# Linear attention on one Trainium2 core: normalising the queries with channels on partitions instead of tokens on partitions

## The chip, the cores and the metric

One core of a Trainium2 chip runs one program. The metric is the device time of the program in microseconds (us), the median of several runs. TensorE (PE) multiplies, VectorE (DVE), ScalarE (ACT) and GpSimd (POOL) work elementwise, and SyncE (SP) issues the DMAs. Each engine executes its own queue in order and waits on semaphores that the others raise.

## The reference

Four layers on x of 1024 tokens and 256 channels, each x + layernorm(layer(layernorm(x))): softmax attention, a mixture of experts, a gated linear attention, and a second mixture of experts. The change is in the linear attention, which has 16 heads of 128 channels:

```
q = silu(causal_dwconv(hidden @ Wq, qconv_w, qconv_b))      # 4 taps
k = silu(causal_dwconv(hidden @ Wk, kconv_w, kconv_b))
q = layernorm(q.reshape(B, L, H, 128), qn_w, qn_b)           # per token and head, over 128 channels
k = layernorm(k.reshape(B, L, H, 128), kn_w, kn_b)
S_t = (1 - b_t) S_(t-1) + b_t v_t k_t^T                      # b_t = sigmoid(hidden @ Wb + bb)
o_t = S_t q_t
out = (o * silu(hidden @ Wg)) @ Wo
```

## The kernel before

The layers follow each other. The linear attention (class `LinearAttention`) takes the span from about 400 to 774 us. It works head by head. The 1024 tokens are 8 tiles of 128 (`NT = 8`), and the recurrence is computed by tiles: inside a tile by scores, from tile to tile by a state of 128 x 128.

The steps of a head h, and the engine of each:

- `high_q`, `high_k`, `high_gate` (ACT) and `low` (POOL) split the float32 weights in two parts; `project_q`, `project_k`, `project_gate`, `project_v` (PE) multiply both parts, so that a projection of 1024 tokens is 12 matmuls of 512 columns (v: 24 of 256).
- `tap` (ACT) copies a projection out of PSUM with the last tap, and `convolve` (DVE) adds the three others in three instructions. Channels are on partitions here. `silu` (ACT) follows.
- `rows_q` and `rows_k` (PE) transpose the eight tiles, so that tokens are on partitions. `variances` (DVE) takes mean and variance of each token; `power` (POOL) makes the inverse deviation.
- For q, `norm_q` (DVE, eight instructions, L2233) subtracts the mean and multiplies by the inverse deviation out of PSUM, `turn_q` (PE, eight transposes) turns the result back to channels on partitions, and `q_transposed` (ACT, L2043) applies weight and bias and writes `q_T`. For k, `shift_k` (DVE) and `norm_k` (ACT, eight instructions) normalise, `rows_k` of POOL (two instructions of 128 x 1024, L2307 and L2309) makes the rows, `turn_k` and `k_transposed` make `k_T`.
- `mask` (POOL) and `exp_mix` (ACT) prepare the decay inside a tile, `decay_q` and `decay_v` (POOL) scale q and v.
- `score`, `key_values`, `outputs` (PE), `probs`, `states` and `gate` (DVE), `silu_gate` (ACT) compute the head's output. `gate` multiplies `outputs` by the gate.

The order on each engine is written out by hand, as a pipeline over steps n in which heads n, n-1 and n-2 are in work. In the steady part a step is:

- PE: rows_q(n-1), turn_k(n-2), rows_k(n-1), project_gate(n-2), score(n-2), key_values(n-2), project_q(n), project_k(n), project_v(n), turn_q(n-1), outputs(n-2).
- DVE: shift_k(n-1), probs(n-2), states(n-2), convolve q(n), convolve k(n), gate(n-2), variances q(n), variances k(n), norm_q(n).
- POOL: power k(n-1), low q(n), low k(n), low v (even n), mask(n), decay_q(n-2), low gate(n-1), rows_k(n-1), decay_v(n-1), power q(n).
- ACT: high_q(n), k_transposed(n-2), high_k(n), silu_gate(n-2), high_v (even n), exp_mix(n-1), tap q(n), norm_k(n-1), tap k(n), high_gate(n-1), silu q(n), q_transposed(n-1), silu k(n), copy_v(n).

Variances of head n run on DVE in step n, but wait for rows_q(n) and rows_k(n), with which PE begins step n+1. Four pairs of PSUM banks hold everything: pair 3 serves project_q, rows_q and turn_q in turn, pair 1 project_k, turn_k and score, pair 2 rows_k and outputs, pair 0 the gate, v and key_values. The wait in front of a PE step is mostly for such a pair. SP loads weights and the decay rows; at step 3 it issues the whole of `Wo` (2 MB), which the next block needs.

## Time and profile before

| what | value |
|---|---|
| median of 3 runs | 1073.07 us (1071.62 to 1076.11) |
| the profiled execution | 1076.29 us, its span 1074.4 us, granted clock 0.984 |
| busy share of the span: PE, DVE, ACT, POOL | 95%, 72%, 63%, 46% |
| from 600 to 750 us, busy of 150 us: PE, DVE, ACT, POOL | 149.46, 137.52, 119.93, 108.71 us |

The profile is one execution, recorded by the hardware. A busy PE is not PE at its peak, since matmuls overlap in the record; whether PE sets the pace is read from what it and the other engines wait for. In a timeline row, "x8" is eight instructions in one row with their time from first start to last end, and the brackets give how long the engine was idle before the row, and what released it.

### The profile page before, as it was taken

What the parts mean: (1) busy time and instruction counts of PE and PEld (TensorE: products, weight loads), DVE (VectorE), ACT (ScalarE), POOL (GpSimd) and SP (SyncE); (2) the same over time, 40 slices, a digit from 0 to 9 for tenths busy, and PEclk for the clock granted to TensorE, in tenths of its full rate; (3) what the DMA queues carried; (4) which work ended last, traced back from release to release, by engine and by line L of the source; (5) the groups of instructions that cost most, each with busy time, mean ns of one, the idle gap of its engine ahead of it and who ended that gap; (6) DMA issues with size and microseconds to landing.
All of it is one profiled execution on the core that took longest, in us unless ns stands there. A gap on an engine that the chain in (4) does not pass through costs nothing. (4 is left out here: it accounts for less than half of the span.)

```text
span 1074.4 us, 19331 instructions
## 1 busy us (share of the span) xinstructions
PE 1024.1 (95%) x6893; PEld 811.8 (76%) x6893; DVE 778.0 (72%) x1645; ACT 675.7 (63%) x1229; POOL 498.5 (46%) x441
## 2 busy tenths in 40 slices
PE   7999999999999996999999999999799999999997
PEld 4333333467888885899899999999699788888997
DVE  5899999556677647899999999999457465343843
ACT  4588888765453447877788788877445353333454
POOL 3351400113079532777767686777306000437443
PEclk9999999999999999899999999999899999999999
DMA  4443434142234103332222123110001123555100
GB/s 97 87 83 51 85 59 70 47 125 73 70 119 93 34 6 117 101 98 64 78 96 65 56 65 114 59 69 21 19 18 42 45 52 97 159 147 171 59 21 20
DMA packets 80794, 79.31 MB, mean 74 GB/s; under 512 B 29384, under 2 KB 67740, under 8 KB 80700
## 3 DMA queue, kind: packets, MB, share of 16 engines
q1 hardware_dynamic: 79968, 77.14, 27.1%
q10 hardware_dynamic: 732, 0.95, 0.3%
q8 instruction: 55, 0.90, 0.3%
q14 instruction: 39, 0.32, 0.1%
HBM read 65.51 MB, written 1.28 MB: 62 GB/s over the span
## 5 line engine op out<-in xcount | busy, mean ns | idle before, releaser
L744 ACT ACTIVATE attn_probs<-attn_rows_k 128x512 f32<-128x512 f32 x256 | 138.9, 595 | 24.1 <-PE attn_rows_k L590 20.9
L590 PE MATMUL attn_rows_k<-attn_q_stack,attn_k_stack 50*128 50x512 f32 x256 | 93.8, 445 | 0.0
L2950 DVE TENSOR_TENSOR late_mids<-late_mids,late_bank 128x512 f32<-128x512 f32 (+1 forms) x50 | 34.3, 686 | 78.4 <-PE late_bank L67 75.4
L855 DVE TENSOR_REDUCE attn_row_max<-s_sum 128x1 f32<-128x1024 f32 x62 | 75.6, 1220 | 10.4 <-PE attn_rows_q L574 5.1
L603 PE MATMUL attn_ctx<-attn_probs,attn_v 128*32 128x256 f32 x1024 | 81.5, 391 | 1.6
L855 DVE TENSOR_REDUCE attn_row_max<-attn_rows_q 128x1 f32<-128x1024 f32 x62 | 75.9, 1224 | 8.6 <-PE attn_rows_q L574 5.2
L65 PE MATMUL late_bank<-net_x_part_low,late_w_T 128*128 128x512 f32 (+1 forms) x192 | 77.9, 406 | 0.0
L66 PE MATMUL late_bank<-net_x_part_low,late_w_T 128*128 128x512 f32 (+1 forms) x192 | 76.1, 396 | 0.0
L67 PE MATMUL late_bank<-net_x_part_low,late_w_T 128*128 128x512 f32 (+1 forms) x192 | 76.0, 396 | 0.0
L2855 ACT ACTIVATE late_mids<-late_bank 128x512 f32<-128x512 f32 (+1 forms) x50 | 29.9, 597 | 69.6 <-PE late_bank L67 69.6
L1611 POOL TENSOR_TENSOR gold_mids<-gold_mids,s_later 128x512 f32<-128x512 f32 x32 | 51.8, 1655 | 46.4 <-DMA s_later<-gold_weights 46.4
L3051 POOL TENSOR_TENSOR late_mids<-late_mids,late_raw_w_T_last 128x512 f32<-128x512 f32 x22 | 29.3, 1352 | 92.3 <-DMA late_raw_w_T_last<-top_weights 92.3
L2203 DVE SCALAR_TENSOR_TENSOR lin_conv_q<-lin_pair,early_lin_taps,lin_conv_q 128x1021 f32<-128x1021 f32 (+2 forms) x48 | 61.4, 1279 | 6.6 <-ACT lin_conv_q L2063 4.2
L2203 DVE SCALAR_TENSOR_TENSOR lin_conv_k<-lin_pair,early_lin_taps,lin_conv_k 128x1021 f32<-128x1021 f32 (+2 forms) x48 | 61.4, 1279 | 2.4
L433 POOL TENSOR_SCALAR attn_max_tok<-attn_row_max 128x8 fp32r<-128x8 f32 x16 | 3.2, 199 | 121.7 <-DVE attn_row_max L855 121.4
L603 PEld LDWEIGHTS attn_ctx<-attn_probs,attn_v 128*32 128x32 f32 x1024 | 20.6, 107 | 46.6 <-ACT attn_probs L744 36.6
L1948 PE MATMUL lin_pair<-lin_probs,lin_v_rows 128*128 128x128 f32 x256 | 48.7, 284 | 4.3 <-DVE lin_state L2195 4.3
L2072 ACT ACTIVATE lin_normed_k<-lin_pair,lin_k_shift,lin_rstd_k 128x128 f32<-128x128 f32 x128 | 46.2, 472 | 1.4 <-DVE lin_k_shift L2175 1.4
L574 PE MATMUL s_sum<-attn_k_stack,attn_q_stack 48*128 48x512 f32 x124 | 45.1, 443 | 1.8 <-DMA attn_q_stack<-s_part 1.4
L65 PE MATMUL late_bank<-late_down_T,late_w_T 128*128 128x256 f32 (+1 forms) x152 | 43.5, 286 | 1.8 <-POOL late_w_T L2650 1.8
L574 PE MATMUL attn_rows_q<-attn_k_stack,attn_q_stack 48*128 48x512 f32 x124 | 45.1, 443 | 0.0
L2840 ACT ACTIVATE late_w_T<-late_mids 128x256 fp32r<-128x256 f32 (+3 forms) x57 | 27.4, 488 | 27.8 <-PE late_bank L67 27.8
(463 smaller groups left out, 3524.1 us busy)
## 6 DMA issues: line engine op xcount, KB each, us to landing
lin_mix<-decay_sums SPq DMA_DIRECT2D x16, 512.0 KB, 3.8
lin_q_dec<-decay_sums SPq DMA_DIRECT2D x16, 512.0 KB, 5.4
s_later<-gold_weights SPq DMA_DIRECT2D x16, 256.0 KB, 3.6
attn_k_stack<-s_part SPq DMA_DIRECT2D x30, 128.0 KB, 3.5
s_raw_ring<-in_L_ffn_Wg SPq DMA_DIRECT2D x12, 256.0 KB, 2.8
s_raw_ring<-in_L_ffn_Wu SPq DMA_DIRECT2D x12, 256.0 KB, 3.1
attn_k_stack<-s_part SPq DMA_DIRECT2D x33, 64.0 KB, 2.3
gold_raw_w_down<-in_L_ffn_Wd SPq DMA_DIRECT2D x1, 2048.0 KB, 12.1
```

The lines of the kernel that those rows point to most:

```text
L65: pe.matmul(out, w[0], x[0], start=start, stop=False)
L66: pe.matmul(out, w[0], x[1], start=False, stop=False)
L67: return pe.matmul(out, w[1], x[0], start=False, stop=stop)
L574: pe.matmul(ps_tile[tile_bank(n)][:, half * HALF:(half + 1) * HALF], q_stack[rows, h % SLOTS, r * P:(r + 1) * P], k_stack[rows, h % SLOTS, ...
L590: pe.matmul(out, k_stack[rows, h % SLOTS, t * P:(t + 1) * P], q_stack[rows, h % SLOTS, :], start=True, stop=True).then_inc(scored_k, 1)
L603: i = pe.matmul(sums[j * VW:(j + 1) * VW, :], v[:, t, h, :], probs[:, (2 * w + odd) % PB, j * QUARTER:(j + 1) * QUARTER], start=(t == 0), ...
L744: act.activation(probs[:, (2 * k + odd) % PB, side * HALF:(side + 1) * HALF], ring_bank(("exped", 4 * k + n + 1)), ACT.Exp).then_inc(exped, 1)
L855: dve.tensor_reduce(row_max[h % 2][:, tile:tile + 1], ps_tile[tile_bank(n)][:, :], axis=AX, op=ALU.max)\
L1611: pool.tensor_tensor(out, out, weight[v % 4], ALU.mult).then_inc(weighted, 1)
L1948: i = pe.matmul(pair[2][:, cols], self.v_rows[h // 2 % 2][:, c, h % 2, :], self.probs[:, c, :], start=True, stop=(c == 0))
L2072: i = act.activation(self.normed[1][:, c, :], self.tiled[2][:, c, :], ACT.Identity, scale=self.rstd[1][:, c:c + 1], bias=self.k_shift[:, c ...
L2203: i = dve.scalar_tensor_tensor(self.conv[m][:, back:T], self.pair[pair][:, 0:T - back], self.taps[:, m, h, j:j + 1], self.conv[m][:, back: ...
```

## The change

q is no longer normalised with tokens on partitions and turned back. The transposed q still gives the statistics. `mean_var` of q (128 x 16: mean and, written over the variance by POOL, inverse deviation) is turned by one transpose into 16 x 128 (`turn_stats`), copied out of PSUM (`copy_stats`, DVE), stored to DRAM (`store_stats`, 8 KB), and loaded back spread to all 128 partitions (`load_norms`, 1 MB). Then q, which stayed as silu wrote it with channels on partitions (`acted`, two buffers), is centred by POOL (`centre_q`) and scaled by DVE (`scale_q`), both 128 x 1024 in place in SBUF, and `q_transposed` reads it from there. On DVE `scale_q(n-1)` stands behind `gate(n-2)`. The second buffer and the loaded rows lie in the space of `Wo`, of which only 4 of 16 parts are loaded at step 3 and the rest when the last q is done. Without `turn_q`, pair 3 is free earlier, and project_gate of the last head moves ahead.

The core of the diff (lines that only rename a buffer or a semaphore are left out):

```
+        def store_stats(h):
+            sp.wait_ge(self.stats_copied, h + 1)
+            sp.dma_start(self.norm_dram[h].rearrange("(r t) -> r t", t=P), self.stat_rows[:, :]).then_inc(self.stats_stored, 16)
+
+        def load_norms(h):
+            sp.wait_ge(self.stats_stored, 16 * (h + 1))
+            if h >= 1:
+                sp.wait_ge(self.q_scaled, h)
+            sp.dma_start(self.norm_rows, self.norm_dram[h:h + 1, :].to_broadcast((P, 2 * T))).then_inc(self.norms_loaded, 16)
+
...
         load_mix(0)
+        store_stats(0)
+        load_norms(0)
         for n in self.STEPS:
             if n == 3:
                 prefetch(sp)
+            if self.live(n - 1) and n > 1:
+                store_stats(n - 1)
+                load_norms(n - 1)
...
+        sp.wait_ge(self.q_T_done, LH)
+        prefetch_rest(sp)
 
...
-        def turn_q(h):
-            pe.wait_ge(self.q_normed, h + 1)
-            if h + 1 < LH:
-                pe.wait_ge(self.q_conved, h + 2)
-            turn(pair[3], lambda c: self.normed[0][:, c, :], self.q_turned)
+        def turn_stats(h):
+            pe.wait_ge(self.q_rstd, h + 1)
+            pe.transpose(pair[3][0:2 * NT, 0:P], self.mean_var[0][:, :, :].rearrange("p c m -> p (c m)"), self.ident[:, :])\
+                .then_inc(self.stats_turned, 1)
 
...
         def project_q(h):
             pe.wait_ge(self.q_split, h + 1)
-            pe.wait_ge(self.q_half_normed, h)
-            self.project_half(pe, "q", 0, pair[3])
-            pe.wait_ge(self.q_normed, h)
-            self.project_half(pe, "q", 1, pair[3]).then_inc(self.q_projected, 1)
+            pe.wait_ge(self.stats_copied, h)
+            project("q", pair[3], self.q_projected)
 
...
         project_k(1)
         rows_k(0)
+        turn_stats(0)
         project_q(1)
-        turn_q(0)
         for n in self.STEPS[2:LH + 1]:
             if live(n - 1):
                 rows_q(n - 1)
@@ -1968,18 +1989,19 @@
                 rows_k(n - 1)
             project_gate(n - 2)
             score(n - 2)
+            if live(n - 1):
+                turn_stats(n - 1)
             key_values(n - 2)
             if live(n):
                 project_q(n)
                 project_k(n)
                 project_v(n)
-            if live(n - 1):
-                turn_q(n - 1)
+            else:
+                project_gate(LH - 1)
             outputs(n - 2)
         turn_k(LH - 1)
         key_values(LH - 1)
         score(LH - 1)
-        project_gate(LH - 1)
         outputs(LH - 1)
 
...
-            act.wait_ge(self.q_turned, h + 1)
+            act.wait_ge(self.q_scaled, h + 1)
             if h >= 1:
                 act.wait_ge(self.scored, h)
                 act.wait_ge(self.q_dec_done, h)
-            act.activation(self.q_T[:, :], self.pair[3][:, :], ACT.Identity, scale=self.norm_col[:, 0:1],
+            act.activation(self.q_T[:, :], self.acted[h % 2], ACT.Identity, scale=self.norm_col[:, 0:1],
                            bias=self.norm_col[:, 1:2]).then_inc(self.q_T_done, 1)
 
...
-        silu(1, 0, self.q_conved, self.q_acted)
+        silu_q(1)
+        silu_k(1)
+        exp_mix(0)
         q_transposed(0)
-        silu(1, 1, self.k_conved, self.k_acted)
-        exp_mix(0)
         for n in self.STEPS[2:LH]:
             if live(n):
                 high_q(n)
             k_transposed(n - 2)
+            if n > 2:
+                q_transposed(n - 2)
             if live(n):
                 high_k(n)
             silu_gate(n - 2)
...
-        def norm_q(h):
-            dve.wait_ge(self.q_rstd, h + 1)
+        def copy_stats(h):
+            dve.wait_ge(self.stats_turned, h + 1)
             if h >= 1:
-                dve.wait_ge(self.q_turned, h)
-            for half, done in ((0, self.q_half_normed), (1, self.q_normed)):
-                for c in range(4 * half, 4 * half + 4):
-                    i = dve.tensor_scalar(self.normed[0][:, c, :], self.tiled[3][:, c, :], self.mean_var[0][:, c, 0:1],
-                                          self.rstd[0][:, c:c + 1], ALU.subtract, ALU.mult)
-                i.then_inc(done, 1)
+                dve.wait_ge(self.stats_stored, 16 * h)
+            dve.tensor_copy(self.stat_rows[:, :], self.pair[3][0:2 * NT, 0:P]).then_inc(self.stats_copied, 1)
+
+        def scale_q(h):
+            dve.wait_ge(self.q_centred, h + 1)
+            q = self.acted[h % 2].rearrange("p (c t) -> p c t", c=NT)
+            dve.tensor_tensor(q, q, self.rstd_rows, ALU.mult).then_inc(self.q_scaled, 1)
 
...
         convolve(1, 0, 3, self.q_tapped, self.q_conved)
         convolve(1, 1, 1, self.k_tapped, self.k_conved)
-        variances(1, 0, 3, self.q_rowed, self.q_rstd, self.q_var)
+        variances(1, 0, 3, self.q_rowed, self.stats_turned, self.q_var)
+        scale_q(0)
         variances(1, 1, 2, self.k_rowed, self.k_rstd, self.k_var)
-        norm_q(1)
         for n in self.STEPS[2:LH + 1]:
             if live(n - 1):
+                copy_stats(n - 1)
+            probs(n - 2)
+            if live(n - 1):
                 shift_k(n - 1)
-            probs(n - 2)
             states(n - 2)
             if live(n):
                 convolve(n, 0, 3, self.q_tapped, self.q_conved)
                 convolve(n, 1, 1, self.k_tapped, self.k_conved)
-            gate(n - 2)
+                gate(n - 2)
+                scale_q(n - 1)
+            else:
+                scale_q(n - 1)
+                gate(n - 2)
             if live(n):
-                variances(n, 0, 3, self.q_rowed, self.q_rstd, self.q_var)
+                variances(n, 0, 3, self.q_rowed, self.stats_turned, self.q_var)
                 variances(n, 1, 2, self.k_rowed, self.k_rstd, self.k_var)
-                norm_q(n)
...
+        def power_q(h):
+            pool.wait_ge(self.q_var, h + 1)
+            pool.tensor_tensor(self.rstd[0], self.var_eps[0][:, :], self.neg_half[:, 0:NT], ALU.pow).then_inc(self.q_rstd, 1)
+
+        def centre_q(h):
+            pool.wait_ge(self.norms_loaded, 16 * (h + 1))
+            q = self.acted[h % 2].rearrange("p (c t) -> p c t", c=NT)
+            pool.tensor_tensor(q, q, self.mean_rows, ALU.subtract).then_inc(self.q_centred, 1)
 
...
             decay_q(n - 2)
             if live(n - 1):
+                centre_q(n - 1)
                 low("gate", self.wg[(n - 1) % 2], self.g_high, self.g_split, n)
                 rows_k(n - 1)
                 decay_v(n - 1)
             if live(n):
-                power(n, 0, self.q_var, self.q_normed, self.q_rstd)
+                power_q(n)
         power(LH - 1, 1, self.k_var, self.k_normed, self.k_rstd)
+        low("gate", self.wg[(LH - 1) % 2], self.g_high, self.g_split, LH)
         decay_q(LH - 2)
-        low("gate", self.wg[(LH - 1) % 2], self.g_high, self.g_split, LH)
         decay_v(LH - 1)
+        centre_q(LH - 1)
         rows_k(LH - 1)
         decay_q(LH - 1)
```

## Rows read from the trace of the kernel before

**Rows 1.** Busy time by stretch (PE, PEld, DVE, ACT, POOL, granted clock, DMA):
```profile
600.00:750.00 150.00, 149.46 (x1049) 137.03 (x1048) 137.52 (x401) 119.93 (x197) 108.71 (x70) 1.00 0.20 69
```
**Rows 2.** Waits from 450 to 750 us: total us, times, longest:
```profile
PEld lin_pair L65 <- POOL lin_part_q L2271: 3.8, 13, 0.5
```
**Rows 3.** Timeline of DVE, one head: start, length, idle before:
```profile
611.19 1.22 DVE L2212 TENSOR_TENSOR s_gated<-s_gated,lin_pair 128x1024 f32<-128x1024 f32 x1 [0.70 <-PE lin_pair L1951]
612.33 1.67 DVE L2218 BATCH_NORM_STATS2 lin_stats_q<-lin_pair 128x6 f32<-128x128 f32 x8
...
617.34 0.17 DVE L2225 TENSOR_SCALAR lin_var_eps_k<-lin_mean_var_k 128x8 f32<-128x8 f32 x1
...
624.41 3.99 DVE L2203 SCALAR_TENSOR_TENSOR lin_conv_q<-lin_pair,early_lin_taps,lin_conv_q 128x1021 f32<-128x1021 f32 x3
...
633.00 1.22 DVE L2212 TENSOR_TENSOR s_gated<-s_gated,lin_pair 128x1024 f32<-128x1024 f32 x1 [0.69 <-PE lin_pair L1951]
```
**Rows 4.** Timeline of POOL, the same head:
```profile
622.88 2.41 POOL L2300 TENSOR_TENSOR lin_q_dec<-lin_q_dec,lin_q_T 128x1024 f32<-128x1024 f32 x1
628.56 0.73 POOL L2271 TENSOR_TENSOR lin_part_gate<-lin_w_gate,lin_part_gate 128x256 fp32r<-128x256 f32 x1 [3.28 <-ACT lin_part_gate L1986]
...
631.77 2.38 POOL L2309 TENSOR_TENSOR lin_k_rows<-lin_k_rows,early_norm_row 128x1024 f32<-128x1024 f32 x1
```
**Rows 5.** Timeline of PE, the same head (PEld: its weight loads):
```profile
619.97 0.19 PEld L65 LDWEIGHTS lin_pair<-net_x_part_low,lin_part_q 128*128 128x128 f32 x1 [0.25 <-POOL lin_part_q L2271]
```
```profile
628.57 1.04 PE L1836 MATMUL lin_pair<-net_ident,lin_normed_q 128*128 128x128 f32 x8
629.45 0.61 PE L1948 MATMUL lin_pair<-lin_probs,lin_v_rows 128*128 128x128 f32 x4
```
**Rows 6.** Timeline of DVE, instructions with two inputs in SBUF:
```profile
298.74 2.31 DVE L1450 TENSOR_TENSOR s_ring_low<-s_raw_ring,s_part 128x1024 fp32r<-128x1024 f32 x1
...
751.25 1.57 DVE L2175 SCALAR_TENSOR_TENSOR lin_k_shift<-lin_mean_var_k,lin_rstd_k 128x8 f32<-128x8 f32 x1
...
779.46 1.22 DVE L2925 TENSOR_TENSOR s_w_o_low<-s_raw_w_o,late_down_T 128x1024 fp32r<-128x1024 f32 x1
```
**Rows 7.** Timeline of POOL at the first two of these:
```profile
297.70 4.50 POOL L1611 TENSOR_TENSOR gold_mids<-gold_mids,s_later 128x512 f32<-128x512 f32 x2
```
```profile
750.44 2.36 POOL L2300 TENSOR_TENSOR lin_q_dec<-lin_q_dec,lin_q_T 128x1024 f32<-128x1024 f32 x1
```
**Rows 8.** DMA issues: count, KB each, median us from issue to landing:
```profile
lin_mix<-decay_sums SPq DMA_DIRECT2D x16, 512.0 KB, 3.8
...
s_raw_ring<-in_L_ffn_Wg SPq DMA_DIRECT2D x12, 256.0 KB, 2.8
...
s_raw_w_o<-in_L_attn_Wo SPq DMA_DIRECT2D x1, 2048.0 KB, 12.2
```
**Rows 9.** Timeline of SP's queue: decay rows stored, then loaded:
```profile
416.54 1.30 SPq L1775 DMA_DIRECT2D decay_sums<-lin_probs  x2
419.43 0.82 SPq L1763 DMA_DIRECT2D lin_mix<-decay_sums  x2
```
**Rows 10.** Timeline of DVE, the first heads:
```profile
422.79 0.17 DVE L2225 TENSOR_SCALAR lin_var_eps_k<-lin_mean_var_k 128x8 f32<-128x8 f32 x1
...
425.31 3.98 DVE L2203 SCALAR_TENSOR_TENSOR lin_conv_q<-lin_pair,early_lin_taps,lin_conv_q 128x1021 f32<-128x1021 f32 x3
...
457.74 1.22 DVE L2212 TENSOR_TENSOR s_gated<-s_gated,lin_pair 128x1024 f32<-128x1024 f32 x1 [0.70 <-PE lin_pair L1951]
```
**Rows 11.** Timeline of PE: third project_q, and outputs(14):
```profile
444.55 0.50 PE L65 MATMUL lin_pair<-net_x_part_low,lin_part_q 128*128 128x512 f32 x1 [0.19 <-POOL lin_part_q L2271]
```
```profile
756.78 1.19 PE L1948 MATMUL lin_pair<-lin_probs,lin_v_rows 128*128 128x128 f32 x4 [4.29 <-DVE lin_state L2195]
```
**Rows 12.** Timeline of DVE, gate(13) and gate(15):
```profile
742.43 1.22 DVE L2212 TENSOR_TENSOR s_gated<-s_gated,lin_pair 128x1024 f32<-128x1024 f32 x1 [0.70 <-PE lin_pair L1951]
```
```profile
773.56 1.22 DVE L2212 TENSOR_TENSOR s_gated<-s_gated,lin_pair 128x1024 f32<-128x1024 f32 x1 [4.05 <-PE lin_pair L1951]
```

More of the change, by code:

```diff
@@ L1651 @@
 LH = 16
+W_O_EARLY = 4
 EARLY_LOADS = 15
@@ L2089, in act @@
         live = self.live
-        tap(0, 0, 3, self.q_projected, self.q_rowed, self.q_tapped)
+        tap(0, 0, 3, self.q_projected, self.q_acted, self.q_tapped)
         high_q(1)
@@ L2119, in act @@
             if live(n):
-                tap(n, 0, 3, self.q_projected, self.q_rowed, self.q_tapped)
+                tap(n, 0, 3, self.q_projected, self.q_acted, self.q_tapped)
             if live(n - 1):
@@ L2127, in act @@
             if live(n):
-                silu(n, 0, self.q_conved, self.q_acted)
-            if live(n - 1):
-                q_transposed(n - 1)
+                silu_q(n)
             if live(n):
-                silu(n, 1, self.k_conved, self.k_acted)
+                silu_k(n)
                 copy_v(n)
         k_transposed(LH - 2)
+        q_transposed(LH - 2)
         silu_gate(LH - 2)
@@ L2138, in act @@
         norm_k(LH - 1)
+        silu_gate(LH - 1)
         q_transposed(LH - 1)
         k_transposed(LH - 1)
-        silu_gate(LH - 1)
     def dve_first(self, dve):
@@ L2213, in gate, with variances @@
                 .then_inc(self.gated, 1)
-        def variances(h, m, pair, rowed, rstd, var):
+        def variances(h, m, pair, rowed, used, var):
             dve.wait_ge(rowed, h + 1)
@@ L2241, in dve @@
         decay_logs()
-        variances(0, 0, 3, self.q_rowed, self.q_rstd, self.q_var)
+        variances(0, 0, 3, self.q_rowed, self.stats_turned, self.q_var)
         mix_biases()
-        norm_q(0)
         variances(0, 1, 2, self.k_rowed, self.k_rstd, self.k_var)
+        copy_stats(0)
         shift_k(0)
@@ L2306, in rows_k @@
             rows = [self.norm_row[:, j, :].rearrange("p (o d) -> p o d", o=1).to_broadcast((P, NT, HD)) for j in range(2)]
-            pool.tensor_tensor(self.k_rows[:, :, :], self.normed[1][:, :, :], rows[0], ALU.mult)
+            pool.tensor_tensor(self.k_rows[:, :, :], self.normed_k[:, :, :], rows[0], ALU.mult)
             pool.drain()
@@ L2329, in pool @@
         low("k", self.wk[1], self.k_high, self.k_split, 2)
-        power(0, 0, self.q_var, self.q_normed, self.q_rstd)
+        power_q(0)
         power(0, 1, self.k_var, self.k_normed, self.k_rstd)
@@ L2334, in pool @@
         mask(0)
-        power(1, 0, self.q_var, self.q_normed, self.q_rstd)
+        centre_q(0)
+        power_q(1)
         mask(1)
```

70 lines of the change are left out of this document (42 added, 28 removed).

## The prediction, written before the change was run

> **What bounds the kernel now.** I looked first at where the change lies: 16 heads, one every 22 us, on one core at full clock. In 150 us of them PE is busy 149.46 us and DVE 137.52 [rows 1], which reads as a PE-bound stretch, in which eight transposes less for each head are a gain. So the second view was what PE waits for, and there it is not alone: before the first matmul of project_q its weight load waits for POOL's `low q`, 3.8 us in 13 heads [rows 2], 0.25 us in the head shown [rows 5]. That small wait is what the reader should follow, because it says which chain sets the period. Followed back through the timelines of DVE, POOL and PE it closes on itself, with no idle time in it:
>
> - gate starts at 611.19, variances q at 612.33 (1.14 us for the gate), variances k end at 617.34 + 0.17 = 617.51 (5.18 us for both) [rows 3];
> - POOL takes the power of k and then `low q`, since its order has them so, and PE begins project_q at 619.97 (2.46 us) [rows 5];
> - project_q, tap q, and convolve q starts at 624.41 (4.44 us) [rows 3];
> - PE goes on with k, v, turn_q and outputs, and the next gate starts at 633.00.
>
> The period is 633.00 - 611.19 = 21.81 us. In its last part DVE convolves q and k until 632.30 and waits 0.70 us for outputs [rows 3]. So PE's pass is 0.70 us behind DVE's convolutions at the gate and 0.25 us ahead of `low q` at project_q: two lanes within a microsecond of each other.
>
> **What is removed.** turn_q stands in the last part of the chain: 629.45 - 628.57 = 0.88 us of PE [rows 5]. Without it outputs end 0.88 us earlier, but the gate can come only 0.70 us earlier, since then DVE is still convolving. norm_q (2.6 us of DVE) stands behind variances k and feeds only turn_q; nothing in the chain waits for it, so its removal gives DVE slack and the period nothing.
>
> **What is added, on the chain.** scale_q stands between gate and variances q, so all of it is on the chain. A DVE instruction of this form (128 x 1024, both inputs in SBUF) took 1.22 us [rows 6], and in a row of instructions 1.14 us from start to start, as the gate does [rows 3]. The period by this alone is 21.81 - 0.70 + 1.14 = 22.25 us, 0.44 us longer.
>
> Then it is held. Two rows show DVE instructions with two SBUF inputs while POOL works in SBUF: a 128 x 8 one took 1.57 us, from 751.25 to 752.82 [rows 6], and POOL's decay_q ran from 750.44 to 752.80 [rows 7]; a 128 x 1024 one took 2.31 us instead of 1.22, and ended at 301.05 with POOL's products under way [rows 6, 7]. The gate never showed this, as one of its inputs is in PSUM. Where will POOL be? Its second instruction of rows_k ends at 631.77 + 2.38 = 634.15 [rows 4], which is 1.85 us behind the end of convolve k at 632.30. Both hang on the same tap and stay so. In the new order the gate starts when convolve k ends; call that 0. scale_q could start at 1.14, POOL is in rows_k until 1.85, so scale_q starts at 1.85: 0.71 us of hold. decay_v is then held by scale_q to 3.0, and still ends near 4.9, before power q is wanted (1.85 + 1.14 + 2.6 = 5.6).
>
> Period: 22.25 + 0.71 = 22.96 us, 1.15 us longer. Gate(0) to gate(13) are 13 periods: 13 x 1.15 = +15.0 us. Bounds: 13 x 0.44 = +5.7 without any hold; above, the next paragraph.
>
> The Trainium skill, page "SBUF — State Buffer", section "Who interferes with whom", states that a DVE instruction with two SBUF inputs and a GpSimd instruction that reads SBUF exclude each other for the whole instruction, whoever issues first going first. The trace agrees as far as rows 6 and 7 go. By that rule the term is +15.0 us, and without it +5.7 us.
>
> **What is added beside the chain.** centre_q costs POOL 2.41 us, the price of decay_q in the same form [rows 4]. POOL waited 3.28 us before `low gate` [rows 4], and centre_q takes that place; it must end 3.74 us before the end of convolve k (632.30 - 628.56), at 22.96 - 3.74 = 19.22, or rows_k and with it the hold move back. So the norms must have landed by 19.2 - 2.4 = 16.8. They come so: variances k end at 1.85 + 1.14 + 5.18 = 8.17; turn_stats ran before (power q ends near 7.35, score near 7); copy_stats ends near 8.5; the store of 8 KB is waited for: the decay rows' stores were issued from 416.54 to 417.84 and the load behind them at 419.43 [rows 9], so 1.6 to 2.9 us, I take 2.2; the load starts at 10.7. For 1 MB there is no row: 256 KB took 2.8 us and 512 KB 3.8 us [rows 8], in line 5.8 us; at most twice the second, 7.6. It lands at 16.5, 0.3 us in time. That is close, and is the second rival.
>
> turn_stats is one transpose in place of eight (0.11 us), on PE in time that it waits for `low q` anyhow; without that cover 0.1 x 13 = 1.4 us. copy_stats (about 0.3 us) and the order of probs and shift_k are covered by DVE's idle time before convolve q, which has the 2.6 us of norm_q added. q_transposed of head n-2 moves behind k_transposed; it ends near 4.8 and score wants it near 5.0, and PE has 1.5 us to spare there. SP now sits in front of its other loads until about 10.7; mix and weights are wanted one step later.
>
> **The start.** project_q(1) ran while DVE was still at head 0. Now it waits for copy_stats, behind variances k of head 0, at 422.79 [rows 10]: it starts near 423.3, and convolve q(1), 4.44 us behind, at 427.8 instead of 425.31, +2.4 us. Then on POOL centre_q(0) stands in front of power q(1), mask(1) and decay_v(0), and q_transposed(0) on ACT behind exp_mix(0); key_values(0) waits for silu_gate(0) behind them. I get project_q(2) near 448.6 instead of 444.55 [rows 11], and the first gate, 0.7 us nearer to it, +3.3 us; PE idles 3 us here, and after 4.29 us of idleness four matmuls took 1.19 us instead of 0.61 [rows 5, 11]: +0.7. Together +4 us; +2 to +8.
>
> **The end.** From gate(13) to gate(15) were 773.56 - 742.43 = 31.13 us [rows 12]. The last head now passes through the store and load with nothing behind it: norms at 16.4, centre_q to 18.8; rows_k's first instruction starts at once and holds scale_q(15) to 21.2; scale_q to 22.4; rows_k ends at 24.7; key_values(15) starts on a PE idle since 17.8, at half rate to 27.8; states and score to about 31; probs to 32.5; outputs (3.4 us) to 36. +5 us; +2 if not held and at full rate, +9 at half rate throughout. The rest of `Wo`, 1.5 MB, goes out at about 23.7; the whole took 12.2 us [rows 8], so it lands by 36, when its third piece is wanted near 37: 0.
>
> **Sum.** 15.0 + 4 + 5 = +24 us. The profiled execution took 1076.29 us, its span 1074.4; it becomes 1100.3. It is 3.22 us above the median of 1073.07, which becomes 1097.
>
> **The rivals.**
>
> A. PE's pass sets the period. For it: 149.46 of 150 us busy, and a wait of only 0.25 us. Then each head saves 0.88 - 0.11 = 0.77 us: 13 x -0.77 = -10, and if start and end cost nothing more, 1063 us. Against it: the chain through `low q` has no gap, and scale_q is in it. It decides if scale_q adds under 0.70 us to the chain. Chance 0.05.
>
> B. The load lands late. By 7.6 us instead of 5.8 it lands 1.5 us too late, rows_k ends at 3.4 instead of 1.85, and the hold grows to 2.2 us: 13 x 2.65 = 34, with start and end +44: 1117 us. For it: only 0.3 us to spare. Chance 0.2, counting smaller delays.
>
> C. scale_q is not held. Then +5.7, start +3, end +2 to 3: +11.5, 1084.5 us. For it: the hold needs POOL to be in rows_k for those 0.7 us, and the rows of it are few. Chance 0.15.
>
> D. Start and end cost nothing and scale_q is short: within 0.5% of before. Chance 0.05.
>
> My forecast has 0.55. The Trainium skill, "DMA: Bandwidth & Descriptors", section "Anatomy of one DMA", prices a DMA at about 2.0 us fixed and the bytes at 436 GB/s; as an estimate that is 4.4 us for the load, which would speak against B; its slope is steeper than these rows show.
>
> **How the numbers follow.** 1097 us. Alone the forecast ranges from 1091 to 1104. The range takes in C and half of B: 1083 to 1113. 0.5% is 5.4 us, about what a measurement of this kernel can tell from no change: faster 0.05 (A), same 0.05 (D), slower 0.9.
>
> **What would show it.** Gates 22.96 us apart (22.25 by C, 21.0 by A, over 23.5 by B). scale_q in the record 1.9 us long, ending with rows_k's second instruction behind it. PE idle 1 to 1.5 us before project_q in each head, for `low q`. centre_q starting within a microsecond of decay_q's end. The forecast is wrong if PE doesn't wait for `low q`, or if POOL is late enough to wait for norms.

## The result and the profile after

The changed kernel took 1093.85 us (median of 4, 1092.78 to 1095.04) beside 1074.59 us for the kernel before on the same chip (median of 4, 1071.62 to 1076.27): 1.018 times as long, 95% interval 1.015 to 1.021, or 19.3 us more. The prediction was 1097.0 us (1083 to 1113), slower. The profiled executions differ by 16.6 us, 1074.4 and 1091.0 us of span, and it is these 16.6 that the rows divide:

| stretch | before, us | after, us | difference | forecast |
|---|---|---|---|---|
| to variances k of head 0 [rows 10] | 422.79 | 421.84 | -0.95 | 0 |
| from there to the first gate [rows 10] | 34.95 | 39.08 | +4.13 | +4 |
| gate(0) to gate(13), 13 periods [rows 10, 12] | 284.69 | 297.36 | +12.67 | +15.0 |
| gate(13) to gate(15) [rows 12] | 31.13 | 33.90 | +2.77 | +5 |
| gate(15) to the end of the span | 300.84 | 298.82 | -2.02 | 0 |
| sum | 1074.4 | 1091.0 | +16.6 | +24 |

The page of the kernel after, busy time of each engine, then the windows view of the stretch of [rows 1] in the same columns:

```profile
PE 1013.5 (93%) x6781; PEld 798.0 (73%) x6781; DVE 772.8 (71%) x1549; ACT 675.0 (62%) x1229; POOL 551.9 (51%) x457
```
```profile
600.00:750.00 150.00, 138.18 (x935) 124.39 (x934) 128.67 (x357) 113.84 (x193) 126.61 (x77) 1.00 0.32 112
```

PE has 11.8 us of idle time in 150 at the same clock, where it had 0.5; DVE has 9 us less to do and POOL 18 more. The waits view from 450 to 765 us says what PE waits for now, against 3.8 us in [rows 2]:

```profile
PEld lin_pair L65 <- POOL lin_part_q L2306: 20.1, 13, 1.9
...
PEld lin_pair L1890 <- POOL lin_mean_var_q L2321: 6.5, 13, 0.9
```

One head in the timelines of DVE, POOL and PE, where [rows 3 to 5] show one of before:

```profile
644.05 1.21 DVE L2241 TENSOR_TENSOR s_gated<-s_gated,lin_pair 128x1024 f32<-128x1024 f32 x1
645.17 1.99 DVE L2265 TENSOR_TENSOR s_raw_w_o<-s_raw_w_o 128x1024 f32<-128x1024 f32 x1
...
652.10 0.17 DVE L2254 TENSOR_SCALAR lin_var_eps_k<-lin_mean_var_k 128x8 f32<-128x8 f32 x1
...
659.08 3.99 DVE L2232 SCALAR_TENSOR_TENSOR lin_conv_q<-lin_pair,early_lin_taps,lin_conv_q 128x1021 f32<-128x1021 f32 x3 [1.66 <-ACT lin_conv_q L2085]
...
666.90 1.21 DVE L2241 TENSOR_TENSOR s_gated<-s_gated,lin_pair 128x1024 f32<-128x1024 f32 x1
```
```profile
643.67 2.41 POOL L2353 TENSOR_TENSOR lin_k_rows<-lin_k_rows,early_norm_row 128x1024 f32<-128x1024 f32 x1
646.03 2.91 POOL L2361 TENSOR_TENSOR lin_v_dec<-lin_v_rows,lin_mix 128x1024 f32<-128x1024 f32 x1
...
656.38 2.42 POOL L2344 TENSOR_TENSOR lin_q_dec<-lin_q_dec,lin_q_T 128x1024 f32<-128x1024 f32 x1
658.74 2.42 POOL L2326 TENSOR_TENSOR lin_acted<-lin_acted,s_raw_w_o 128x1024 f32<-128x1024 f32 x1
663.32 0.73 POOL L2306 TENSOR_TENSOR lin_part_gate<-lin_w_gate,lin_part_gate 128x256 fp32r<-128x256 f32 x1 [2.17 <-ACT lin_part_gate L2008]
```
```profile
654.73 0.50 PE L65 MATMUL lin_pair<-net_x_part_low,lin_part_q 128*128 128x512 f32 x1 [1.33 <-POOL lin_part_q L2306]
```

The period is 666.90 - 644.05 = 22.85 us (forecast 22.96). scale_q (L2265) is 1.99 us long in the record and 1.92 from its start to the next; POOL's second rows_k ends at 646.08, and a multiplication of 1.2 us that starts there ends at 647.2, as this one does. It is so in all 14 heads from 1 to 14: scale_q ends 1.08 or 1.09 us behind the end of rows_k. The 1.92 us stand in the chain: variances k end 8.22 us behind the gate (6.32 in [rows 3]), project_q starts at 10.68 (8.78 in [rows 5]), convolve q at 15.03 (13.22), and the next gate follows convolve k with no idle time.

The load of the norms, in SP's timeline and in the DMA issues:

```profile
652.51 0.33 SPq L1781 DMA_DIRECT2D query_norms<-lin_stat_rows  x1
653.87 0.33 SPq L1787 DMA_DIRECT2D s_raw_w_o<-query_norms  x1
```
```profile
s_raw_w_o<-query_norms SPq DMA_DIRECT2D x16, 1024.0 KB, 4.9
```

The store is waited for 1.36 us, the load takes 4.9 (the median of all 16): it lands 14.7 us behind the gate, about when decay_q ends. centre_q starts with no idle time in front of it, and 2.17 us are left before `low gate`. Not every head is so. The store is waited for 1.35 to 1.37 us in ten heads of 16 and up to 3.37 us in the others, and in six heads between 450 and 765 us POOL waits for the norms, 4.6 us in all. The longest of these waits, in POOL's timeline:

```profile
569.14 2.41 POOL L2326 TENSOR_TENSOR lin_acted<-lin_acted,s_raw_w_o 128x1024 f32<-128x1024 f32 x1 [2.11 <-DMA s_raw_w_o<-query_norms]
```

This centre_q starts 16.84 us behind its gate (at 552.30), and the next gate still comes after 22.85 us.

The last heads, in DVE's, POOL's and PE's timelines:

```profile
758.28 1.21 DVE L2241 TENSOR_TENSOR s_gated<-s_gated,lin_pair 128x1024 f32<-128x1024 f32 x1
...
775.48 3.36 DVE L2265 TENSOR_TENSOR s_raw_w_o<-s_raw_w_o 128x1024 f32<-128x1024 f32 x1 [3.83 <-POOL s_raw_w_o L2326]
...
792.18 1.22 DVE L2241 TENSOR_TENSOR s_gated<-s_gated,lin_pair 128x1024 f32<-128x1024 f32 x1 [3.71 <-PE lin_pair L1972]
```
```profile
773.09 2.36 POOL L2326 TENSOR_TENSOR s_raw_w_o<-s_raw_w_o 128x1024 f32<-128x1024 f32 x1
775.40 2.35 POOL L2351 TENSOR_TENSOR lin_k_rows<-lin_normed_k,early_norm_row 128x1024 f32<-128x1024 f32 x1
777.90 3.15 POOL L2353 TENSOR_TENSOR lin_k_rows<-lin_k_rows,early_norm_row 128x1024 f32<-128x1024 f32 x1
```
```profile
781.15 3.33 PE L1956 MATMUL lin_pair<-lin_v_dec,lin_k_rows 128*128 128x128 f32 x14 [4.69 <-issue]
```

scale_q(15) is held for the whole first instruction of rows_k, and holds the second in its turn (3.15 us instead of 2.4). key_values(15) then runs at about half its rate: behind 4.69 us without work, PE's granted clock is 0.50 from 781.15 to 784.27, the lower of its two levels (1.2 GHz of 2.4).

### The profile page after: what moved, and what is told of

Its sections match the earlier page's. It is cut to its first block and busy times, and to the rows that moved or that the text cites. A ratio compares the mean times of both kernels' runs of the same rounds, so it can differ in the third digit from the quotient of the medians.

```text
span 1091.0 us, 19044 instructions
## 1 busy us (share of the span) xinstructions
PE 1013.5 (93%) x6781; PEld 798.0 (73%) x6781; DVE 772.8 (71%) x1549; ACT 675.0 (62%) x1229; POOL 551.9 (51%) x457
## 5 line engine op out<-in xcount | busy, mean ns | idle before, releaser
L855 DVE TENSOR_REDUCE attn_row_max<-s_sum 128x1 f32<-128x1024 f32 x62 | 75.6, 1220 | 10.9 <-PE attn_rows_q L574 5.2
L603 PEld LDWEIGHTS attn_ctx<-attn_probs,attn_v 128*32 128x32 f32 x1024 | 20.6, 107 | 46.8 <-ACT attn_probs L744 36.7
L2085 ACT ACTIVATE lin_conv_q<-lin_pair,early_lin_taps 128x1024 f32<-128x1024 f32 x16 | 19.3, 1207 | 53.3 <-PE lin_pair L67 53.3
L65 PE MATMUL lin_pair<-net_x_part_low,lin_part_q 128*128 128x512 f32 x64 | 27.9, 435 | 20.5 <-POOL lin_part_q L2306 17.6
```

The source lines that it names most:

```text
L65: pe.matmul(out, w[0], x[0], start=start, stop=False)
L603: i = pe.matmul(sums[j * VW:(j + 1) * VW, :], v[:, t, h, :], probs[:, (2 * w + odd) % PB, j * QUARTER:(j + 1) * QUARTER], start=(t == 0), ...
L855: dve.tensor_reduce(row_max[h % 2][:, tile:tile + 1], ps_tile[tile_bank(n)][:, :], axis=AX, op=ALU.max)\
```

## The experiments

Eleven edits and one repetition, each timed in turns with the kernel before on its chip. "Period" is the mean of the 13 periods from gate(0) to gate(13); it is 21.90 us in the kernel before and 22.87 in the kernel after.

| run | time, us | to before | period, us |
|---|---|---|---|
| e5, before, one transpose of turn_q | 1065.42 | 0.991 (0.989 to 0.993) | 21.41 |
| e2, after without scale_q | 1071.26 | 0.998 (0.995 to 1.000) | 21.31 |
| e1, after, scale_q on 128 x 8 | 1079.7 | 1.004 (1.001 to 1.006) | 21.85 |
| e6, after, norms last on SP | 1134.5 | 1.055 (1.053 to 1.058) | 26.00 |
| e3, after, low q first | 1076.36 | 1.000 (0.998 to 1.002) | 21.46 |
| e4, before, low q first | 1080.62 | 1.005 (1.002 to 1.008) | 22.36 |
| e8, e4 and shift_k on POOL | 1067.46 | 0.994 (0.992 to 0.996) | 21.49 |
| e10, after, both ends mended | 1090.82 | 1.017 (1.012 to 1.022) | 22.86 |
| e11, e3 and the start mended | 1070.73 | 0.996 (0.994 to 0.998) | 21.43 |
| e7, e3 and both ends mended | 1068.34 | 0.994 (0.992 to 0.996) | 21.47 |
| e12, e7 again | 1071.78 | 0.996 (0.994 to 0.999) | 21.39 |
| e9, e7 and shift_k on POOL | 1073.43 | 0.998 (0.996 to 1.000) | 21.62 |

**The removed part alone (e5).** Seven of the eight transposes of turn_q are left out of the kernel before.

```
-            turn(pair[3], lambda c: self.normed[0][:, c, :], self.q_turned)
+            pe.transpose(pair[3][:, 0:P], self.normed[0][:, 0, :], self.ident[:, :]).then_inc(self.q_turned, 1)
```

> The kernel before with one of the eight transposes of turn_q (the seven others are left out, so seven tiles of q_T are not the queries). This is the removed part alone, with nothing added. My theory: PE is 0.77 us shorter a head, but the gate can come only 0.70 us earlier, since DVE's pass stands right behind it: gates 21.1 us apart, 13 x 0.70 = 9 us less, 1066 us against 1075.5. Rival, PE's pass was not on the chain at all: no change. This bounds what the change could have brought.

The time is as expected, the period is not: it is 0.49 us shorter and not 0.70, 6.4 of the 9.6 us won. In the profiles, which differ by 10.9 us, the rest is 2.5 us ahead of gate(0), 1.0 from gate(13) to gate(15) and 1.1 behind. One thing that the expectation left out is a new hold, in every second head, in DVE's and POOL's timelines:

```profile
608.80 0.37 DVE L2225 TENSOR_SCALAR lin_var_eps_q<-lin_mean_var_q 128x8 f32<-128x8 f32 x1
```
```profile
607.23 1.92 POOL L2317 TENSOR_TENSOR lin_v_dec<-lin_v_rows,lin_mix 128x1024 f32<-128x1024 f32 x1 [0.29 <-issue]
```

This addition takes 0.17 us in the kernel before; here it ends with POOL's decay_v. The change starts from a real gain, and the added work eats it.

**The added multiplication (e2 and e1).** e2 takes scale_q out of the changed kernel, with q_transposed and the next load of norms behind centre_q. e1 lets it stand, with its place and its wait, on 8 columns instead of 1024:

```
-            q = self.acted[h % 2].rearrange("p (c t) -> p c t", c=NT)
-            dve.tensor_tensor(q, q, self.rstd_rows, ALU.mult).then_inc(self.q_scaled, 1)
+            q = self.acted[h % 2][:, 0:8]
+            dve.tensor_tensor(q, q, self.rstd_rows[:, 0, 0:8], ALU.mult).then_inc(self.q_scaled, 1)
```

> The kernel after without scale_q at all (q is centred and not scaled; q_transposed and the next load of the norms wait for centre_q instead). My theory: 1.85 us leave the chain in every head, of which 1.14 are work and 0.7 hold; gates 21.0 to 21.1 us apart, 13 x 1.8 = 23 us less, and about 1 us more at the end, 1069 us. This is what the removal of turn_q alone would be worth with everything else in place. Rival, PE or the wait for the norms sets the period of the kernel after: less than half of it, above 1082 us.

> The kernel after, with scale_q cut from 128 x 1024 to 128 x 8 elements, still with both inputs in SBUF and in the same place (so most of q is left unscaled). My theory: scale_q is on the chain that sets the period, and it waits there until POOL's second rows_k instruction ends, whatever its own size. Then its row stays 0.7 to 0.9 us long, the gates stand 21.8 to 21.9 us apart instead of 22.84, and the time is about 1080 us. Rival, no hold (the 1.97 us of scale_q are its own, from its operands): the row shrinks to 0.2 us, the gates stand 21.2 us apart, about 1072 us. Rival, scale_q is not on the chain: no change.

Without scale_q the period is 21.31 us (the forecast's 21.81 - 0.70 = 21.11, and most single ones are 21.1 to 21.35), and the time falls by 22.6 us, more than the whole loss. In e1, DVE's timeline and POOL's at one head:

```profile
615.28 0.91 DVE L2265 TENSOR_TENSOR lin_acted<-lin_acted,s_raw_w_o 128x8 f32<-128x8 f32 x1
```
```profile
613.77 2.39 POOL L2353 TENSOR_TENSOR lin_k_rows<-lin_k_rows,early_norm_row 128x1024 f32<-128x1024 f32 x1
```

Eight columns take 0.91 us, and end where POOL's instruction ends (616.16); in all 14 heads they end 0.02 to 0.04 us behind it, and at head 0, where they don't meet rows_k, they take 0.17 us. The hold is there whatever the size of the multiplication: a single period is typically 21.77 us here, and the other 22.84 - 21.77 = 1.07 us are the work of the 1024 columns.

**Where the load stops being hidden (e6).** SP issues store and load of the norms behind the other loads of its step.

```
-            if self.live(n - 1) and n > 1:
-                store_stats(n - 1)
-                load_norms(n - 1)
             if 2 <= n + 1 < LH:
                 load_qk(n + 1)
...
             if self.live(n - 1):
                 load_decay(n - 1)
+            if self.live(n - 1) and n > 1:
+                store_stats(n - 1)
+                load_norms(n - 1)
```

> The kernel after with the store and the load of the norms issued behind the step's other loads on SP instead of ahead of them. My theory of the hold says that the load has some 1.2 us to spare (centre_q starts 16.3 us behind the gate, the norms land near 15.1), and that every microsecond beyond moves rows_k, and with it the end of the hold on scale_q, by as much. The issue moves back by some 3 us and the load then runs among 1.75 MB of others: I expect landing near 20 us, gates 24.5 to 26 us apart, and 1115 to 1135 us. Rival, the load is hidden and only PE's and DVE's passes count: no change, 1094 us.

The period is 26.0 us, and centre_q waits for the load (POOL's timeline of this run):

```profile
642.91 2.37 POOL L2326 TENSOR_TENSOR lin_acted<-lin_acted,s_raw_w_o 128x1024 f32<-128x1024 f32 x1 [6.62 <-DMA s_raw_w_o<-query_norms]
```

Rival B is a real mechanism and not what happened. The store is waited for 4.8 us here (issued at 633.16, the load at 637.95) against 1.36 with nothing in front, so the place in SP's order carries the change.

**The chain through POOL (e3 and e4).** `low q(n)` goes ahead of power k(n-1) on POOL, in both kernels.

```
+                if live(n):
+                    low("q", self.wq[n % 2], self.q_high, self.q_split, n + 1)
                 power(n - 1, 1, self.k_var, self.k_normed, self.k_rstd)
             if live(n):
-                low("q", self.wq[n % 2], self.q_high, self.q_split, n + 1)
```

> The kernel after with POOL's low q(n) in front of power k(n-1) instead of behind it. My theory: the chain then no longer passes through variances k and the power of k on its way to project_q; project_q waits for key_values or copy_stats, near 9.1 us behind the gate instead of 10.6, and the gates stand 21.5 us apart: 13 x 1.35 = 17.5 us less, about 1076 us. Rival, the period is set by PE's pass or by DVE's pass and low q is only the last of several waits: less than 0.3 us a head, 1090 us or more.

> The kernel before with the same exchange on POOL. My theory: project_q's wait of 0.25 us for low q goes, and PE's pass of 21.5 to 21.6 us sets the period: 13 x 0.22 = 3 us less, about 1071 us against 1074. If the wait was an artefact of the record, or something else stands right behind it: no change.

In the changed kernel it gives back 17.5 us (18.4 by the 13 periods): variances k and power k leave the chain, and PE's 20.1 us of waits for `low q` go. This shows that the chain through `low q` set the period of the changed kernel. With the shorter period the norms are late in one head, which rival B describes; DVE's and POOL's timelines of e3:

```profile
589.41 3.21 DVE L2265 TENSOR_TENSOR s_raw_w_o<-s_raw_w_o 128x1024 f32<-128x1024 f32 x1
```
```profile
583.60 2.38 POOL L2326 TENSOR_TENSOR s_raw_w_o<-s_raw_w_o 128x1024 f32<-128x1024 f32 x1 [1.25 <-DMA s_raw_w_o<-query_norms]
```

rows_k is late with centre_q, scale_q is held to 591.54, and that period is 22.49 us. In the kernel before it costs 5 us where I had expected a gain, a miss. DVE's timeline and POOL's show why:

```profile
622.40 1.19 DVE L2175 SCALAR_TENSOR_TENSOR lin_k_shift<-lin_mean_var_k,lin_rstd_k 128x8 f32<-128x8 f32 x1
```
```profile
622.27 1.30 POOL L2271 TENSOR_TENSOR lin_part_v<-early_lin_w_v,lin_part_v 128x512 fp32r<-128x512 f32 x1
```

Power k is later, so shift_k (L2175, two inputs in SBUF) now asks just behind the start of POOL's `low v` and is held: 1.19 us instead of 0.63, and in the heads without `low v`, behind the start of `mask`, 0.98. The mean of both, 0.46 us more, is what the period grew by (22.36 - 21.90). DVE's pass gets longer, convolve q starts 13.79 us behind the gate instead of 13.22, and PE waits for it before turn_q. So DVE's pass was as tight as the chain through `low q` all along, which the prediction had not said.

**The held shift_k taken away (e8).** In e4, shift_k becomes two short instructions of POOL right behind power k.

```
+        def pool_shift(h):
+            pool.drain()
+            pool.tensor_tensor(self.k_shift[:, :], self.mean_var[1][:, :, 0], self.rstd[1][:, :], ALU.mult)
+            pool.drain()
+            pool.tensor_scalar(self.k_shift[:, :], self.k_shift[:, :], -1.0, None, ALU.mult).then_inc(self.shift_ready, 1)
```

> The kernel before with low q ahead of power k, and k's shift made by two short POOL instructions right behind power k instead of by DVE. The same exchange alone made the kernel before 5 us slower: DVE's shift_k (128 x 8, both inputs in SBUF) came 0.1 us behind the start of POOL's low v or mask and was held 1.0 to 1.2 us instead of 0.6. My theory: with no such instruction on DVE, nothing is held, DVE's pass gets 0.6 us of slack, and PE's pass of 21.5 to 21.6 us sets the period: 3 us less than before, 1072 us. Rival, the loss came from low k being later and not from the hold: still 1080 us.

The period is 21.48 or 21.49 us in 12 heads of 13, in the mean 0.87 less than in e4, and the time is 1067.46 us, 4.5 better than expected: the reading of e4 holds, since no instruction but the held one was moved. The old normalisation of q, with this order, is faster than the kernel before by 0.6% (medians 1067.46 and 1075.05 us). The two POOL instructions take 0.20 and 0.24 us.

**The two ends (e10, e7, e9, e11, e12).** The start: turn_stats(0) writes to pair 0, and project_q(1) waits for variances q(0) instead of copy_stats(0). The end: centre_q(15) behind rows_k(15), k_transposed(15) ahead of q_transposed(15), gate(14) ahead of scale_q(15).

```
-            pe.wait_ge(self.stats_copied, h)
+            pe.wait_ge(self.stats_copied if h >= 2 else self.q_var, h)
...
         decay_v(LH - 1)
-        centre_q(LH - 1)
         rows_k(LH - 1)
+        centre_q(LH - 1)
```

> The changed kernel with only the two ends mended: turn_stats(0) goes to pair 0 and project_q(1) waits for variances q(0) alone; for head 15 centre_q stands behind rows_k, k_transposed before q_transposed, and gate(14) before scale_q(15). Power k still stands before low q in each step. Theory (start and end are costs of their own beside the period): the period stays 22.84 us, the first gate comes 1.5 to 3 us earlier, gate(13) to gate(15) falls from 33.90 to about 31.6 us, and the time is 1088 to 1091 us, 3 to 6 us under the changed kernel. Rival (the start catches up by itself, since the first full step waits for something else): only the end's 2.3 us are won, 1091.5 us or more, with the first gate at 460.5 to 461.

> The kernel after with low q ahead of power k, and its start and end mended: the statistics of head 0 are turned into pair 0 of PSUM, so that project_q(1) waits only for variances q(0); for the last head centre_q stands behind rows_k, k_transposed ahead of q_transposed, and gate(14) ahead of scale_q. My theory: the start costs 3 us more than before and the end 2.8 us, and these edits give back 2.5 and 3 of them: 1071 us against 1076.4 of the same kernel without them and 1075.5 before. Rival, the start and the end hang on other waits (POOL's centre_q(0), the load of the last norms): 1075 us or more.

> The mended kernel of the earlier run (low q first, turn_stats and project_q of head 1 unhooked, centre_q and scale_q of the last head moved) and besides shift_k on POOL, as two short instructions behind power k. In the run with low q first DVE had no idle time but 0.41 us before shift_k, which took 0.62 us more to the next start, in a period of 21.46 us. Theory (DVE's pass with scale_q in it sets that period, and PE's pass of about 21.0 us is right under it): the period falls by 0.4 to 0.5 us to about 21.0, 13 periods give back 5 to 6 us, and the time is 1062 to 1065 us, the shortest of all. Rival (norms' load, which left 0.8 us to spare before low gate, is now late, and the hold by rows_k grows by as much as DVE gained): period 21.3 to 21.5, time 1067 to 1070 us, and POOL waits for the load of norms in each head.

> The changed kernel with low q first and the start mended, the end as the change has it (centre_q before rows_k). The run with only the two ends mended had its first gate 2.8 us earlier and nothing back at the end (gate(13) to gate(15) 34.14 us against 33.90). Theory (the start is worth 2.8 us, the end's mending nothing): period 21.46 us as with low q first alone, gate(13) to gate(15) 33.9 us, time 1076.4 - 2.8 = 1073.5 us (1071 to 1075). Rival (the end's mending pays once low q stands first, as the first run of the mended kernel, 1068.3 us, would have it): this kernel is 2 to 5 us slower than the mended one, at 1073 or more, and the mended one is at 1068 to 1070 again.

> The mended kernel once more, unchanged, because its first profile lay 22 us late as a whole and its terms could not be read from it. Theory (the end's mending is worth nothing): gate(13) to gate(15) is 33.5 to 34.5 us and the time 1071 to 1074 us, as the kernel without that mending. Rival: gate(13) to gate(15) is 31.6 us again and the time 1068 to 1070 us.

The start can be read without what came before it, from variances k(0) to the first gate. In e10, DVE's timeline:

```profile
423.55 0.17 DVE L2258 TENSOR_SCALAR lin_var_eps_k<-lin_mean_var_k 128x8 f32<-128x8 f32 x1
...
458.11 1.21 DVE L2245 TENSOR_TENSOR s_gated<-s_gated,lin_pair 128x1024 f32<-128x1024 f32 x1
```

That is 34.56 us, as in e11 and e12, against 39.08 in the kernel after and 34.95 before: the start's whole loss is the wait of project_q(1) for copy_stats(0), 4.5 us and not the 1.5 to 3 expected (this execution was 1.7 us later where the stretch begins, so the gate itself came only 2.8 earlier). e11 was expected at 1073.5 us from these 2.8 us; it took 1070.73, and its first gate is 4.8 us ahead of e3's. e10's time lies in the range that was expected, but its ratio of 1.017 (1.012 to 1.022) can't be told from the changed kernel's 1.018.

The mended end gains nothing in these profiles, where 2.3 us were expected. Where the changed kernel takes 33.90 us from gate(13) to gate(15), e10 takes 34.14, and e12 35.61 beside 33.28 of e11, which lacks it. The order did what it was meant to do. DVE's timeline of e12 shows scale_q(15) at its full speed:

```profile
756.45 1.23 DVE L2269 TENSOR_TENSOR s_raw_w_o<-s_raw_w_o 128x1024 f32<-128x1024 f32 x1 [3.43 <-POOL s_raw_w_o L2330]
```

key_values(15) starts 19.8 us behind gate(13) in e10 instead of 22.9, and takes 1.80 us; q_T comes 2.7 us later, and score(15), which needs q_T and stands behind key_values on PE, starts at 24.6 instead of 26.0. What is won there PE's clock takes back. score(15) and the first matmuls of outputs(15), in PE's timelines of the kernel after and of e10:

```profile
784.27 2.59 PE L1945 MATMUL lin_pair<-lin_q_T,lin_k_T 128*128 128x128 f32 x16
...
788.53 0.71 PE L1969 MATMUL lin_pair<-lin_probs,lin_v_rows 128*128 128x128 f32 x4 [1.67 <-DVE lin_probs L2212]
```
```profile
779.92 3.13 PE L1949 MATMUL lin_pair<-lin_q_T,lin_k_T 128*128 128x128 f32 x16 [3.00 <-ACT lin_q_T L2069]
784.37 1.22 PE L1973 MATMUL lin_pair<-lin_probs,lin_v_rows 128*128 128x128 f32 x4 [1.32 <-DVE lin_probs L2216]
```

From the start of score(15) to gate(15) the windows view has, for the kernel after, e10 and e12:

```profile
784.27:792.18 7.91, 6.20 (x47) 5.82 (x46) 3.51 (x8) 0.00 (x0) 0.00 (x0) 0.92 0.30 93
```
```profile
779.92:789.49 9.57, 8.22 (x46) 7.73 (x46) 2.40 (x5) 0.00 (x0) 2.35 (x1) 0.64 0.54 165
```
```profile
759.00:769.78 10.78, 9.42 (x46) 8.93 (x46) 2.41 (x6) 0.00 (x0) 2.35 (x1) 0.57 0.46 147
```

In the kernel after PE is slow in key_values(15) and at full clock again for outputs(15); in e10 and e12 it is slow in score(15) and in a part of outputs(15). So these profiles don't show that the mending is worth nothing: it was measured at another clock. In the first profile of the mended kernel (e7) the clock is 1.00 from score(15) on, the same stretch takes 7.02 us, and gate(13) to gate(15) takes 31.56, as expected; but this execution was 22 to 24 us later than the others before it reached the stage, and it is one. Whether the mended end pays in most executions stays open. The times say as little: e7's 1068.34 us and its repetition's 1071.78 were measured apart, and e11's 1070.73 beside the second. Whether e7 or e11 is faster stays open; both are faster than the kernel before.

In e9 both theories fell. The period, expected near 21.0 or at 21.3 to 21.5 us with POOL waiting for the norms in each head, has a mean of 21.62, and POOL waits for the norms in three heads. The single period is mostly 21.25 and 21.95 us in turn, though DVE has 1.2 us to spare before convolve q. In every second head POOL does `low v` as well (1.3 us), and with shift_k on it too it is late with rows_k; its timeline and DVE's in such a head:

```profile
590.64 2.39 POOL L2361 TENSOR_TENSOR lin_k_rows<-lin_k_rows,early_norm_row 128x1024 f32<-128x1024 f32 x1
```
```profile
590.21 1.21 DVE L2245 TENSOR_TENSOR s_gated<-s_gated,lin_pair 128x1024 f32<-128x1024 f32 x1
591.34 2.78 DVE L2269 TENSOR_TENSOR s_raw_w_o<-s_raw_w_o 128x1024 f32<-128x1024 f32 x1
```

scale_q is held to 593.03 and takes 2.78 us. With the changed kernel's POOL full, what is moved there comes back as a longer hold on DVE.

Two ways lead below both kernels, about equally far: the old normalisation with e8's order (0.994), and the new one with low q first and the start mended (0.996, 0.994 in e7). The new normalisation as such therefore wins nothing that these runs can tell.

## Why the prediction was right

The change was slower by the mechanism that was forecast: scale_q in the chain through `low q`, and held there by POOL's rows_k. Of the smaller terms, the start came out right by luck, and the end was sized wrong.

**The chain.** "Two lanes within a microsecond of each other": right for PE and `low q`, and the step that carried the forecast. e3 shows it, by 17.5 us. A third lane, DVE's own pass through shift_k, states and convolve q, was missed; it changed nothing here, since the chain through `low q` grew past both, but it made e4's expectation wrong.

**scale_q in the chain, 1.14, and held, 0.71 us.** Measured 1.92 together, forecast 1.85. e1 shows the hold by itself and e2 the whole. The rule of the Trainium skill, page "SBUF — State Buffer", section "Who interferes with whom", that such a DVE instruction and one of GpSimd exclude each other for the whole instruction, agrees with the trace in heads 1 to 14 of the kernel after and of e1: scale_q ends 1.08 us, one multiplication, or 0.02 us behind the end of rows_k.

**The removed part, -0.70.** e2's shortest and most frequent periods, 21.08 to 21.11 us, are 0.70 under the 21.81 of the kernel before. In e5, where the part was taken out alone, the mean fell by 0.49 only.

**The period, 22.96, and its 13 times 1.15 = 15.0.** The single period came out at 22.85, the term at 12.67. Of the 2.3 us less, 13 x (22.96 - 22.87) = 1.2 are the new period, whose mean is 22.87. The other 13 x (21.90 - 21.81) = 1.2 are my base: 21.81 us was one head, and the mean, 284.69 / 13, was 21.90, from two rows that I had in hand. The lengthening is 0.97 us for each head and not 1.15.

**The load, in time by 0.3 us.** In time by 2.1 us in the head shown: the store is waited for 1.36 us (I took 2.2) and the load takes 4.9 (5.8, on the line through two smaller ones). The line was too steep, at 4 us for each MB. In the slowest head nothing was to spare: centre_q started at 16.84 where 16.8 was the limit. So "POOL is late enough to wait for norms", which the prediction gave as a sign of being wrong, did come in six heads, and the period didn't show it. The Trainium skill, "DMA: Bandwidth & Descriptors", section "Anatomy of one DMA", gives 4.4 us as an estimate; the trace lies between. That section is on DMAs issued by GpSimd, and SP issues this one. The prediction calls its slope steeper than the rows; as an estimate, 436 GB/s are 2.4 us for each MB, which is flatter.

**The start, +4.** Measured +4.13, and e10 and e11 put it on the first cause named, project_q(1) behind copy_stats(0). The rest of the sum is luck. I had 2.4 us at convolve q(1), 0.9 from the later orders of POOL and ACT, and 0.7 for a slower PE. From variances k(0) to convolve q(1) the kernel after takes 7.02 us where the kernel before took 2.52 [rows 10], which is 4.5 by itself, and from there to the first gate 0.4 us less than before. What I took too low is project_q(1): it starts 0.5 us behind variances k as forecast, but after 2.90 us without work, and at a granted clock of 0.50 its matmuls are 0.63 us long where 0.40 is their length at full clock. In PE's and DVE's timelines of the kernel after:

```profile
422.34 0.77 PE L65 MATMUL lin_pair<-net_x_part_low,lin_part_q 128*128 128x512 f32 x1 [2.90 <-DVE lin_stat_rows L2260]
```
```profile
428.86 3.99 DVE L2232 SCALAR_TENSOR_TENSOR lin_conv_q<-lin_pair,early_lin_taps,lin_conv_q 128x1021 f32<-128x1021 f32 x3 [4.41 <-ACT lin_conv_q L2085]
```

**The end, +5.** Measured +2.77, the worst term. The norms landed 14.8 us behind gate(13) at the latest instead of 16.4, and every step behind them came as much earlier: scale_q ended at 20.6 (22.4), rows_k at 22.8 (24.7), the last gate at 33.9 (36). The hold and the half rate of key_values were as forecast. This is the same mis-sized load as above. The half rate costs 1.5 us (3.33 us instead of 1.80): in e11, with the same order at the end and key_values at 2.72 us, the end is shorter by the same 0.6 us. The kernel before had its own slow PE there, in outputs(14) [rows 11]. So the difference of 2.77 us hangs on the clock as well as on the way of the norms.

**What the sum left out.** The late block took 2.0 us less. It is the clock: in the 12 us behind gate(15) PE was granted 0.86 in the kernel after and 0.72 before (windows view: after, before, then e11 and e12), while it was busy for the same 8.8 us:

```profile
792.18:804.18 12.00, 8.76 (x60) 8.76 (x61) 8.79 (x12) 7.29 (x12) 0.00 (x0) 0.86 0.27 80
```
```profile
773.56:785.56 12.00, 8.76 (x50) 8.77 (x51) 8.22 (x11) 6.08 (x11) 0.00 (x0) 0.72 0.25 79
```
```profile
767.77:779.77 12.00, 8.77 (x61) 8.77 (x62) 8.81 (x12) 7.27 (x12) 0.00 (x0) 0.86 0.28 80
```
```profile
769.78:781.78 12.00, 8.77 (x52) 8.77 (x53) 8.22 (x11) 6.35 (x11) 0.00 (x0) 0.72 0.28 79
```

e11 and e12 have the same two values, and late blocks of 298.7 and 300.7 us, so this is worth the 2 us. The 14 profiles agree: where this value is 1.00 (e7, e10) the late block takes 297.4 and 297.8 us, where it is 0.86 (four runs) 298.7 to 299.8, and where it is 0.72 (the other eight) 299.9 to 300.8. Why the full clock returned sooner in one than in another was not tried.

**The rivals.** A fell by e2: PE's pass without scale_q is 21.1 to 21.3 us, and the kernel is 1.5 above it. B is real (e6, and one head of e3) and was 2.1 us away in the head shown (14.7 against the 16.8 that centre_q has), and not at all in the slowest. C fell by e1. The range held the time.

## What to carry to other kernels

Before a transpose or any work is moved off the busiest engine, follow the chain that sets the period through all engines, and ask which added instruction stands in it: here 0.88 us of PE went and 1.9 us of DVE came. A multiplication with two inputs in SBUF beside a busy POOL costs the rest of POOL's instruction whatever its own size, so work moved to POOL has to be counted on both engines. Take the period as a mean over all heads, compare short stretches of two single profiles only with their granted clock beside them, and change the order of two instructions only after looking at what each of them will then meet.

## What the runs showed of the hardware

- The hold doesn't need a big instruction: 128 x 8 took 0.91 us (e1) and 1.19 (e4). Nor two tensors: the addition of a constant to 128 x 8, 0.17 us in most heads, took 1.08 in e10 beside POOL's centre_q, which ran from 435.05 to 437.40, and 1.45 in the kernel before beside decay_v (from 440.64 to 442.09, decay_v to 442.05):

```profile
436.34 1.08 DVE L2258 TENSOR_SCALAR lin_var_eps_q<-lin_mean_var_q 128x8 f32<-128x8 f32 x1
```

- It goes the other way too: POOL's power of 128 x 8 took 2.66 us instead of 1.65 while DVE's scale_q ran (e10: from 437.50, scale_q at 437.43), and decay_v 2.91 us instead of 1.92.
- DVE gets its turn at the border between two instructions of POOL, and POOL's next one then waits: in the kernel after rows_k ends at 646.08, scale_q at 647.16, and decay_v, which starts at 646.03 in the record, takes 2.91 us.
- After 4.69 us without work PE did 14 matmuls of 128 x 128 in 3.33 us at a granted clock of 0.50; in the head before they took 1.79 at 1.00.
- A load that waits for a store of 8 KB is issued 1.36 us behind it in ten heads of 16 and up to 3.37 us in the others, with no issue just in front of it (kernel after), and 4.3 to 6.4 us with the step's other loads in front (e6).
